# 64-wide attention of a two-layer kernel: TensorE reads the turned rows of x in their own buffer instead of a copy, and one turn of probabilities goes ahead of a turn of keys

## The reference

```
x = x + _L0_attn_ref(_layernorm(x, axis=-1), ...)      # linear attention with decay, 16 heads
x = x + _L0_ffn_ref(_layernorm(x, axis=-1), ...)       # gated feed-forward with Hadamard transforms
x = x + _L1_attn_ref(_layernorm(x, axis=-1), ...)      # softmax attention, 16 heads of 16 (4 for keys)
x = x + _L1_ffn_ref(_layernorm(x, axis=-1), ...)       # causal attention with 64-wide heads, then a mixture of experts
```

```
h = _rms(x, ln_w)
q = (h @ wq).reshape(B, S, NHEADS, HEAD_DIM)           # 32 query heads of 64
k = (h @ wk).reshape(B, S, KVHEADS, HEAD_DIM)          # 8 key heads of 64
v = (h @ wv).reshape(B, S, KVHEADS, HEAD_DIM)
q, k = _rope(q, k)
scores = jnp.einsum('bqhd,bkhd->bhqk', q, k) / np.float32(np.sqrt(HEAD_DIM))
scores = jnp.where(causal[None, None], scores, jnp.float32(-1e+30))
attn = jax.nn.softmax(scores, -1)
o = jnp.einsum('bhqk,bkhd->bqhd', attn, v).reshape(B, S, NHEADS * HEAD_DIM)
x = x + o @ wo
```

## Time and profile before

| | before |
|---|---|
| median of three runs | 2106.87 us (2105.41 to 2108.44) |
| the profiled execution | 2098.91 us |
| its span | 2097.1 us |
| TensorE busy | 1796.6 us (86%) |
| VectorE busy | 1291.1 us (62%) |
| ScalarE busy | 1095.7 us (52%) |
| GpSimd busy | 902.6 us (43%) |
| the copies of `stage` | 32, from 799.6 to 1678.1 us |

### The profile page before, as it was taken

One profiled execution on the slowest core, in us unless ns is written; L12 is line 12 of the kernel. 1 busy time (PEld: TensorE's weight loads), 2 busy tenths in 40 slices (PEclk: granted clock), 3 DMA queues, 4 the chain that ended last, 5 costly groups with the idle time before them and its releaser, 6 DMA issues.

```text
span 2097.1 us, 32365 instructions
## 1 busy us (share of the span) xinstructions
PE 1796.6 (86%) x10666; PEld 1213.7 (58%) x10666; DVE 1291.1 (62%) x3898; ACT 1095.7 (52%) x2886; POOL 902.6 (43%) x1013
## 2 busy tenths in 40 slices
PE   4989899857888855999999999999999993799994
PEld 2656688723434323666666666666666663555552
DVE  5775545446686855777777777777777767522222
ACT  3323344226565533676667667666776661344441
POOL 3991000002222001555555455554554552588884
PEclk9999899958999986999999999999999995899997
DMA  5000020000001010000000000000000007354556
GB/s 153 1 1 1 1 61 1 1 0 1 1 1 41 1 43 1 1 1 1 1 1 1 1 1 1 1 1 1 1 1 1 1 1 245 106 84 83 83 83 164
DMA packets 61426, 61.71 MB, mean 29 GB/s; under 512 B 13136, under 2 KB 58320, under 8 KB 61264
## 3 DMA queue, kind: packets, MB, share of 16 engines
q0 software_dynamic: 15360, 20.98, 6.3%
q1 hardware_dynamic: 45904, 38.65, 5.7%
HBM read 40.48 MB, written 19.14 MB: 28 GB/s over the span
## 4 chain that ended last, share of the span: by engine, by line
PE 55%; DVE 21%; ACT 10%; issue 8%; POOL 4%; DMA 2%; SPq 0%; ACTq 0%; POOLq 0%; DVEq 0%
PE banks L1818 7%; PE banks L1808 5%; PE banks L1799 4%; PE banks L1787 4%; PE banks L1777 3%; DVE wide_x L1052 3%; PE banks L1995 3%; PE banks L1621 3%; PE banks L1872 3%; PE banks L1830 2%; POOL wdT L725 2%; PE banks L1847 2%; DVE con L1063 2%; PE banks L1683 2%; ACT attn L1419 2%
## 5 line engine op out<-in xcount | busy, mean ns | idle before, releaser
L1777 PE MATMUL banks<-wide_k,wide_q 128*128 128x512 f32 (+3 forms) x1024 | 307.4, 382 | 4.7 <-DVE con L1037 1.9
L1406 ACT ACTIVATE wugT<-wugT,con 128x512 f32<-128x512 f32 (+1 forms) x256 | 169.7, 664 | 126.8 <-DVE con L1037 126.6
L657 POOL TENSOR_TENSOR wugT<-wugT,con 128x512 f32<-128x512 f32 (+1 forms) x256 | 232.8, 935 | 2.5 <-DVE con L1016 2.5
L668 POOL TENSOR_TENSOR attn<-attn 128x320 f32<-128x320 f32 x128 | 111.3, 870 | 267.4 <-DVE attn L1004 267.4
L1037 DVE CUSTOM_DVE_ANT_0 wugT<-banks,wide_mask 128x512 f32<-128x512 f32 (+1 forms) x256 | 158.0, 617 | 98.7 <-PE banks L1777 94.7
L1818 PE MATMUL banks<-late,xnT 128*128 128x384 f32 x512 | 195.1, 505 | 10.9 <-ACT xnT L1436 9.7
L1777 PEld LDWEIGHTS banks<-wide_k,wide_q 128*128 128x128 f32 x1024 | 166.9, 190 | 59.1 <-DVE con L1037 24.1
L1063 DVE TENSOR_REDUCE con<-banks 128x1 f32<-128x512 f32 x256 | 163.6, 680 | 52.5 <-PE banks L1860 52.1
L1799 PE MATMUL banks<-attn 128*64 128x256 f32 x1280 | 166.4, 389 | 0.0
L1995 PE MATMUL banks<-w,late 128*128 x320 | 156.2, 611 | 2.6 <-ACT late L1533 1.9
L1237 DVE TENSOR_TENSOR late<-late,banks 128x256 f32<-128x256 f32 x80 | 33.7, 421 | 195.8 <-ACT late L1543 177.9
(11 more groups left out here) (311 smaller groups left out, 4174.5 us busy)
## 6 DMA issues: line engine op xcount, KB each, us to landing
w<-in_L_ffn_w_dram SPq DMA_DIRECT2D x32, 256.0 KB, 5.5
late<-in_L_ffn_w_dram SPq DMA_DIRECT2D x16, 256.0 KB, 5.8
y_rows<-wqkv1T SPq DMA_DIRECT2D x1, 2176.0 KB, 7.9
x<-in_L_attn_x_dram SPq DMA_DIRECT2D x4, 512.0 KB, 9.0
late<-in_L_ffn_wq_dram SPq DMA_DIRECT2D x2, 1024.0 KB, 7.3
late<-in_L_ffn_wo_dram SPq DMA_DIRECT2D x1, 2048.0 KB, 9.2
h_rows<-wugT SPq DMA_DIRECT2D x1, 2048.0 KB, 7.0
y_rows<-x SPq DMA_DIRECT2D x1, 2048.0 KB, 13.2
```

What stands on the lines that cost most here:

```text
L657: nc.gpsimd.tensor_tensor(p, p, rinv[:, m:m + 1].to_broadcast([P, n]), ALU.mult).then_inc(at.sem["norm"], 1)
L1406: nc.scalar.activation(at.prob(m)[:, 0:n], at.prob(m)[:, 0:n], ACT.Exp, bias=negmax[:, m:m + 1], scale=-1.0, accum_out=rowsum[:, m:m + 1]) ...
L1777: ins = nc.tensor.matmul(sbank[:, 0:keys], wide_q[:, side, i, qcols], wide_k[:, side, w, 0:keys], start=(w == 0), stop=(w == 1))
```

## The change

The entry `stage` goes, with its semaphore, its ScalarE copy and TensorE's wait for it. The products of `qkv` take the turned rows out of `wide_xT`, at the place of the round's sequence and the tile. In slot 13 the entries ("turn_qk", 1, 5) and ("turn", 0, 6) change places.

```diff
-        WIDE = {0: [("stage", 1, 0), ("turn", -1, 8)],
+        WIDE = {0: [("turn", -1, 8)],
...
-                13: [("turn_qk", 1, 5), ("turn", 0, 6)],
+                13: [("turn", 0, 6), ("turn_qk", 1, 5)],
...
-            ops = [("stage", 0, 0)]
+            ops = []
...
-                    elif kind == "stage":
-                        if reached(n):
-                            act.wait_ge(at.sem["qkv_ps"], n * TB)
-                        nc.scalar.activation(xnT[:], all_xT[:, :, bass.ds(b(n) * S, S)], ACT.Copy).then_inc(at.sem["stage"], 1)
...
                     elif kind == "qkv":
-                        if a == 0:
-                            pe.wait_ge(at.sem["stage"], n + 1)
                         if reached(n_y):
                             pe.wait_ge(at.sem["yb"], n_y - spare)
+                        first = S * sequence_of(n) + P * wide_tile(a)
                         for c in range(DC):
-                            ins = nc.tensor.matmul(at.ybank("qkv", a)[:, 0:QKV], xnT[:, c, P * wide_tile(a):P * wide_tile(a) + P], w_qkv(n, c),
+                            ins = nc.tensor.matmul(at.ybank("qkv", a)[:, 0:QKV], wide_xT[:, c, first:first + P], w_qkv(n, c),
                                                    start=(c == 0), stop=(c == DC - 1))
```

More of the change, by code:

```diff
@@ L288, in two_layers @@
         class Attention:
-            names = ("xT_ps", "xT_dve", "xT_act", "stage", "qkv_ps", "rope", "yb", "sum", "hi", "qk", "m_ps", "m_sb", "s_ps",
+            names = ("xT_ps", "xT_dve", "xT_act", "qkv_ps", "rope", "yb", "sum", "hi", "qk", "m_ps", "m_sb", "s_ps",
                      "max", "exp", "inv", "norm", "t_ps", "pt_dve", "pt_act", "v", "pv", "o_sb", "y_ps")
```

## The result

| | before | after |
|---|---|---|
| median of 5 runs each, same chip | 2108.44 us (2105.41 to 2112.34) | 2089.71 us (2085.89 to 2095.95) |
| the profiled execution | 2098.91 us | 2085.89 us |
| its span | 2097.1 us | 2084.1 us |

The ratio is 0.9914 (95%: 0.9897 to 0.9931): 18.7 us less. The forecast was 19.5 us less. From here on "before" and "after" stand for the two kernels.

What follows compares the result with a forecast made beforehand. The prediction took TensorE, busy 95% of the steady rounds, to bound the kernel. Its terms, 15.6 + 2.8 + 1.15 = 19.5 us, taken from 2106.87 us gave 2087.4 us, range 2083 to 2093.

Steps and rivals of the forecast that it cites:

- The wait for the copy: Steady rounds, `qkv` 0 behind scores 1: without TensorE's wait for `stage`, 0.52 us a round gained, 15.6 us in all.
- rival B: Steady rounds: only the idle bracket of 0.26 us a round comes back; 2095.1 us, chance 0.11.
- Nothing else late behind it: Behind `qkv` 0: rotation and next items move with it; no other engine holds that place, VectorE keeps 0.23 us of slack.
- Rival C: The wait comes back elsewhere, TensorE idling 0.52 us longer in slot 13; 2102.9 us, no change, chance 0.10.
- The swap: Slot 13: `turn` 6 ahead of `turn_qk` 5 lets `turn_qk` 6 start 0.09 us earlier a round, 2.8 us in all.
- Rival A: Slot 13: exchanging the two entries gives all of its 0.38 us a round; 2078.4 us, chance 0.10.
- The prologue: Prologue: without the copy, TensorE's first `qkv` starts 0.14 us behind the last write of `wide_xT`, gaining 1.15 us.
- Rival D: Slot 4: VectorE's `low` pair grows from 1.10 to 2.04 us beside GpSimd's products; slower, 2116.5 us, chance 0.07.

Runs made afterwards that it cites:

- only_read: After, with slot 13 in its old order (`turn_qk` 5 ahead of `turn` 6); 2090.43 us, ratio 0.993, 27.772 us a round.
- only_swap: Before, with only the two entries of slot 13 exchanged; 2103.99 us, ratio 0.9985, 28.313 us a round.
- copy_kept: After, with ScalarE still making the rounds' 31 copies, which nobody reads or waits for; 2090.42 us, ratio 0.9922, 27.782 us a round.
- long_before: Before, with the copy of `turn_qk` 5 split into two ScalarE instructions so that it ends later; 2109.49 us (one run), 28.373 us a round.
- proj_first: After, with `project` 0 ahead of `turn_qk` 6 in slot 14; 2092.63 us, ratio to before 0.9947, 27.927 us a round.
- all_three: After, with `project` 0 ahead of `turn_qk` 6, `turn_qk` 7 behind `values` 4 and 5, `turn_qk` 4 ahead of `values` 2 and 3; 2069.27 us, ratio 0.9842.
- prologue_copy: After, with one 128 x 1024 ScalarE copy behind the last write of `wide_xT`, awaited by TensorE before its first `qkv`; 2093.91 us (one run).
- prologue_busy: As prologue_copy, but TensorE also turns six tiles that nobody uses ahead of that wait; 2102.14 us (one run).
- proj_late7: After, with `project` 0 ahead of `turn_qk` 6 and `turn_qk` 7 behind `values` 4 and 5; 2084.48 us, ratio 0.9917, 27.567 us a round.
- long_after: After, with the copy of `turn_qk` 5 split into two ScalarE instructions; 2081.88 us (one run), 27.842 us a round.

## Why the prediction was right

The sign and the main cause were right; one small term was wrong, and one was missed. That the total came within 1 us is luck, as the two nearly cancel. By its steps:

- *The wait for the copy, 0.52 us a round.* Right: 0.53 us (only_read against before) or 0.52 us (after against only_swap), and the two spacings came as read, 0.55 and 1.28 us. With it falls rival B, which had only the idle bracket of 0.26 us. copy_kept shows that it is the wait and not the copy's own time.
- *Nothing else late behind it.* Right. VectorE's wait before the rotation fell to 0.22 us (0.23 predicted). Rival C falls: TensorE's idle time in slots 13 and 14 went from 0.99 to 0.86 us.
- *The swap, 0.09 us a round.* Wrong: 0. The step that failed is "with the 0.06 us from a copy's end to the turn `turn_qk` 6 starts at 1220.80". I took that 0.06 us from `turn_qk` 5, and it doesn't hold for `turn_qk` 6. Behind the copy of `turn_qk` 5 the lag is 0.15 us in before (1220.74 to 1220.89) and 0.14 us in after (1212.77 to 1212.91), where the wait is seen. So `turn_qk` 6 was bound to that copy already, which long_before shows from outside, and there was no room to win. Why the lag differs isn't settled. It isn't how long TensorE idled: `turn_qk` 7 in proj_first (0.45 us idle) and `turn_qk` 5 in all_three (no bracket) start 0.05 us behind their copies, too. Rival A falls with it.
- *The prologue, 1.15 us.* The wait was right to the hundredth, with the 0.14 us of lag as predicted. Missed: another 2.16 us, since TensorE idled 0.87 instead of 2.02 us there and kept its clock at 2.4 GHz. The row was in front of me: a first `qkv` of 2.60 us in the earlier trace rows against 1.45 us in the earlier trace rows. prologue_copy and prologue_busy show the cause, one run each, and all the other traces agree with them. The Trainium skill (TensorE: Matmul & The Clock Gate, section What's actually happening) says that the array's full clock is not its default but is released by recent activity. By that rule the traces agree: 2.54 us behind 2.02 us of idle time, 1.56 us behind six turns and 0.21 us of it. I had not asked what a shorter idle stretch would give back.
- *Rival D.* It falls: the `low` pair of slot 4 took 1.10 us, as before. VectorE and GpSimd moved together: GpSimd's products start 1.86 us behind the rotation, before 1.85 us.

The two errors, 2.8 us too much and 2.2 us too little, nearly cancel; the steady rounds were 0.3 us too high. The sum of 19.5 stands against 18.6 in the trace and 18.7 in the medians. The total is no proof of its terms: without the swap's 2.8 us the same sum would have been 16.7 us and the forecast 2090.1 us, also within the range of 2083 to 2093.

## What to carry to other kernels

What a wait costs is read from the spacing of the same instructions where they don't wait, not from the idle bracket; and a wait can bind without any bracket, so before moving work into idle time ask what the *next* instruction of the same bank or buffer waits for, and how long a chain turn, copy, turn is by itself. Here such a chain didn't get cheaper by work put behind one link (proj_first lost 0.13 us a round), but by work behind two (0.23 gained) and an earlier first link as well (0.50 gained). The row of the weight load can show a wait that the row of the matmul hides. Where an idle stretch of TensorE shrinks, compare the lengths of the same instructions behind it with rows at the full clock, for the clock may give more than the wait, as it did in this prologue.

## What the runs showed of the hardware

- In this prologue 2.02 us of idle TensorE go with a first `qkv` within which the clock falls to the lower level (2.54 to 2.60 us in before, only_swap, long_before and prologue_copy; the granted clock over it was 0.56 in before and 0.57 in prologue_copy), and 0.87 us with one at the full clock (1.53 us in after, only_read, copy_kept, proj_first, proj_late7, all_three and long_after).
- From the end of a ScalarE copy to the start of the TensorE instruction that waits for it: 0.05 to 0.06 us for `turn_qk` 5 and, in proj_first, `turn_qk` 7; 0.14 to 0.15 us for `turn_qk` 6 and for the prologue's `qkv`.
- A TensorE instruction that binds on a copy can show no idle time: with 0.07 us added to the copy its start moved by 0.06 us, with no bracket in either trace. In all_three the matmul row of `turn_qk` 5 has no bracket, while its weight load has one of 0.22 us for the copy.
